# Order of the work ahead of the first group of a four-layer attention kernel: weight loads without a wait, buffer clears moved, step list rewritten

## What is computed

```python
x = L0(x, ctx)   # normalise rows, project with Wn, Wm, Wl (64x64) and biases bn, bm, bl; softmax over 256 positions;
                 # Wo, bo; + x
x = L1(x, ctx)   # layer norm of ctx (gamma, beta), Q K V, 16 heads of 16, softmax over 64, Wo, times tanh(gate), + x
x = L2(x, ctx)   # the same with its own weights
x = L3(x, ctx)   # q = x Wq^T, k, v from ctx, one head of 256, softmax over 64, Wo, times alpha, + x
```

## Time and profile before

| | before |
|---|---|
| median of 3 runs | 714.7 us (714.55 to 716.21) |
| profiled execution, device time | 714.7 us |
| its span in the profile | 712.5 us |
| PE busy | 652.5 us (92%) |
| PE weight loads busy | 578.6 us (81%) |
| DVE busy | 494.7 us (69%) |
| ACT busy | 463.4 us (65%) |
| POOL busy | 203.7 us (29%) |

### The profile page before, as it was taken

How to read it: one execution, slowest core, us unless ns; L and a number is a source line. 1 busy time by engine, 2 the same in 40 slices (tenths; PEclk the granted TensorE clock), 3 DMA queues, 4 the chain that set the end, 5 groups by cost and what they waited for, 6 DMA issues and landing times.

```text
span 712.5 us, 21646 instructions
## 1 busy us (share of the span) xinstructions
PE 652.5 (92%) x8643; PEld 578.6 (81%) x8643; DVE 494.7 (69%) x1083; ACT 463.4 (65%) x893; POOL 203.7 (29%) x169
## 2 busy tenths in 40 slices
PE   2988999989999899989999899998999899998985
PEld 1867898778988799878987789877988789987884
DVE  5857687675777657685776757867577857765575
ACT  1886575865847666665757658486575666676571
POOL 6333610426006250145203370061601533021100
PEclk9999999999999999999999999999999999999999
DMA  6320000200002000200003000020001100000000
GB/s 154 119 63 2 3 2 2 95 2 2 2 31 65 1 2 2 93 4 2 2 2 94 2 2 2 20 77 2 2 2 48 48 2 1 2 33 2 2 2 30
DMA packets 18491, 18.18 MB, mean 26 GB/s; under 512 B 1829, under 2 KB 18341, under 8 KB 18405
## 3 DMA queue, kind: packets, MB, share of 16 engines
q1 hardware_dynamic: 17504, 16.42, 7.3%
q0 software_dynamic: 320, 0.26, 0.4%
q10 hardware_dynamic: 580, 0.14, 0.1%
HBM read 12.63 MB, written 4.19 MB: 24 GB/s over the span
## 4 chain that ended last, share of the span: by engine, by line
PE 45%; issue 26%; POOL 12%; ACT 8%; DVE 4%; DMA 3%; ACTq 1%; SPq 1%; POOLq 0%; DVEq 0%
PE psum L352 7%; PE psum L561 7%; PE psum L354 6%; PE psum L353 5%; PE psum L581 4%; PE psum L634 4%; POOL kbd L1113 3%; ACT work L755 3%; PE psum L437 2%; POOL x_norm L1154 2%; ACT work L741 2%; POOL c_norm L1154 2%; PE psum L627 2%; PE psum L571 1%; ACT v L694 1%
## 5 line engine op out<-in xcount | busy, mean ns | idle before, releaser
L1113 POOL TENSOR_TENSOR kbd<-k_tmp,own_row 128x1024 f32<-128x1024 f32 x32 | 60.6, 1893 | 400.4 <-ACT k_tmp L689 400.4
L922 DVE TENSOR_REDUCE negmax<-psum 128x8 f32<-128x512 f32 x128 | 87.6, 684 | 35.2 <-PE psum L561 35.2
L755 ACT ACTIVATE work<-psum,group_mask 128x512 f32<-128x512 f32 x128 | 80.2, 688 | 28.0 <-PE psum L581 27.8
L926 DVE TENSOR_TENSOR shifted<-psum,negmax 128x512 f32<-128x512 f32 x128 | 88.5, 692 | 8.0 <-ACT work L741 2.9
L741 ACT ACTIVATE work<-shifted 128x512 f32<-128x512 f32 x128 | 77.6, 632 | 13.8 <-DVE shifted L926 13.5
L581 PE MATMUL psum<-const,work 64*128 64x64 f32 x1536 | 67.0, 228 | 17.8 <-ACT work L741 15.6
L581 PEld LDWEIGHTS psum<-const,work 64*128 64x128 f32 x1536 | 55.6, 139 | 32.7 <-issue 29.3
L561 PE MATMUL psum<-kbd,work 64*128 64x128 f32 x1024 | 71.5, 282 | 3.9 <-POOL kbd L1113 2.1
L634 PE MATMUL psum<-v,work 128*64 128x34 f32 x2048 | 69.2, 225 | 5.7 <-ACT work L755 5.7
L634 PEld LDWEIGHTS psum<-v,work 128*64 128x64 f32 x2048 | 64.2, 138 | 12.0 <-issue 10.7
L561 PEld LDWEIGHTS psum<-kbd,work 64*128 64x128 f32 x1024 | 61.7, 188 | 10.7 <-ACT work L706 2.8
(11 more groups left out here) (182 smaller groups left out, 1705.9 us busy)
## 6 DMA issues: line engine op xcount, KB each, us to landing
x_raw<-in_x_dram SPq DMA_DIRECT2D x8, 512.0 KB, 3.9
c_raw<-in_ctx_dram SPq DMA_DIRECT2D x8, 512.0 KB, 4.7
out_dram<-attn SPq DMA_DIRECT2D x16, 256.0 KB, 2.7
mrow_u<-in_mask_dram SPq DMA_DIRECT2D x8, 64.0 KB, 4.6
work<-in_L_xattn_Wq_dram SPq DMA_DIRECT2D x2, 256.0 KB, 4.1
work<-in_L_xattn_Wk_dram SPq DMA_DIRECT2D x2, 256.0 KB, 4.4
work<-in_L_xattn_Wv_dram SPq DMA_DIRECT2D x2, 256.0 KB, 5.0
work<-in_L_xattn_Wo_dram SPq DMA_DIRECT2D x2, 256.0 KB, 6.0
```

The source lines that it names most:

```text
L755: act.activation(probsT[:, slot, :], o[:], ACT.Copy, scale=group_mask[:, i:i + 1]).then_inc(free, 1)
L922: dve.tensor_reduce(negmax[:, i % 2, :], sv, AX_X, ALU.max, negate=True).then_inc(rowmax, 1)
L926: dve.tensor_tensor(shifted[:, i % 2, :].rearrange("t (j k) -> t j k", k=C), sv, negmax[:, i % 2, :].unsqueeze(2).broadcast_to([P, NJ, C]) ...
L1113: pool.tensor_tensor(kbd[l - 1][:, i], k_tmp[:, i, :].rearrange("p (b s) -> p b s", s=C).unsqueeze(2).broadcast_to(each), own_row[:].unsqu ...
```

## The change

Four things are changed, all in the start. SP no longer waits at L331. ACT's queue issues the four weights of layer 0 ahead of the three bias rows. DVE clears `v2`, `probs3` and `v0` at its very beginning, directly behind `w0_bd`, and not behind `MV`. And `PROLOGUE` lists the same steps in another order, which also gives many steps another bank.

```diff
-    o = p("MT") + [("ST", 0)] + p("GT") + [("ST", 1)] + [("ST", 2)] + p("MS") + [("ST", 3)] + [("MV", 0)] + f("xT", 0)
-    o += [("WB", 0)] + [("NB", 0)] + f("cT", 0) + f("cT", 1) + p("Wq1", "Wk1") + [("NM", 1)] + [("TG", 0)] + p("W0T")
-    o += [("NM", 0)] + p("Wv1", "Wo1") + f("xT", 1) + p("Wq2") + f("nT", 0) + f("nT", 1) + f("Mn", 0) + p("Wo3T")
-    o += f("Mn", 1) + p("Wk2", "W0", "Wv2", "Wo2") + f("Mm", 0) + [("KB", 1)] + p("M3") + f("V0", 0) + f("V0", 1)
-    o += [("KB", 2)] + f("Mm", 1) + p("VW3", "VB2", "VB1") + [("OB", 1)] + [("OB", 2)]
+    o = p("MT", "MS") + [("ST", 0)] + [("ST", 1)] + f("cT", 0) + f("xT", 0) + [("ST", 2)] + [("ST", 3)] + [("MV", 0)]
+    o += p("GT") + f("xT", 1) + [("WB", 0)] + p("Wq1", "Wk1") + [("NB", 0)] + [("TG", 0)] + f("cT", 1) + p("W0T", "Wv1")
+    o += [("NM", 1)] + p("Wq2", "Wk2") + [("NM", 0)] + p("Wo1", "Wv2", "W0") + [("KB", 1)] + f("nT", 0) + f("nT", 1)
+    o += p("Wo2", "Wo3T", "M3") + f("Mn", 0) + f("Mn", 1) + f("Mm", 0) + f("V0", 0) + [("KB", 2)] + p("VB1") + [("OB", 1)]
+    o += f("Mm", 1) + f("V0", 1) + p("VW3", "VB2") + [("OB", 2)]
...
             load_group(0)
-            sp.wait_ge(w0_bias_loaded, 3 * 16)
-            sp.wait_ge(w0_loaded, 4 * 16)
             for n in "qkvo":
...
+            for i, n in enumerate(("Wn", "Wm", "Wo", "Wl")):
+                act.dma_start(w0_raw[:, i, :], w[f"L0_xattn_{n}"].unsqueeze(0).broadcast_to([2, C, C])).then_inc(w0_loaded, 16)
             for i, n in enumerate(("bn", "bm", "bl")):
...
-            for i, n in enumerate(("Wn", "Wm", "Wo", "Wl")):
...
             dve.memset(w0_bd, 0.0).then_inc(w0_ready, 1)
+            for t in (v2[0], v2[1], probs3):
+                dve.memset(t[:], 0.0)
+            dve.memset(v0[:, :, :, C], 1.0).then_inc(cleared, 1)
...
                     moments_step(None)
-                    clear_values()
```

More of the change, by code:

```diff
@@ L825, in _ @@
                               w[f"L0_xattn_{n}"].unsqueeze(0).unsqueeze(0).broadcast_to([1, 2, C])).then_inc(w0_bias_loaded, 16)
-            for i, n in enumerate(("Wn", "Wm", "Wo", "Wl")):
-                act.dma_start(w0_raw[:, i, :], w[f"L0_xattn_{n}"].unsqueeze(0).broadcast_to([2, C, C])).then_inc(w0_loaded, 16)
             for step in PROLOGUE:
@@ L1053, in iteration @@
                         moments_step(g)
-            def clear_values():
-                for t in (v2[0], v2[1], probs3):
-                    dve.memset(t[:], 0.0)
-                dve.memset(v0[:, :, :, C], 1.0).then_inc(cleared, 1)
-                dve.wait_ge(cleared, 1)
-                for t in v2:
-                    for h in range(2):
-                        dve.memset(t[C * h:C * h + C, :, :, h, VW - 1], 1.0).then_inc(cleared, 1)
-            dve.memset(w0_bd, 0.0).then_inc(w0_ready, 1)
+            dve.memset(w0_bd, 0.0).then_inc(w0_ready, 1)
+            for t in (v2[0], v2[1], probs3):
+                dve.memset(t[:], 0.0)
+            dve.memset(v0[:, :, :, C], 1.0).then_inc(cleared, 1)
+            dve.wait_ge(cleared, 1)
+            for t in v2:
+                for h in range(2):
+                    dve.memset(t[C * h:C * h + C, :, :, h, VW - 1], 1.0).then_inc(cleared, 1)
             dve.wait_ge(mask_loaded, 16)
```

## The result

| | before | after |
|---|---|---|
| median | 714.6 us (714.34 to 716.21, 4 runs) | 722.1 us (721.12 to 726.43, 4 runs) |
| ratio to before | | 1.0113, 95% interval 1.0077 to 1.0151 |
| profiled execution, its span | 714.7 us, 712.5 us | 722.0 us, 720.0 us |

The change made the kernel slower by 1.1%; the prediction was 711.3 us, with a range from 710.0 to 717.0. What happened is the first rival, the starving bias rows, and further than its own end, 718.8.

What follows compares the result with a forecast made beforehand. Bound: ACT's queue in the start's second half, begun behind DVE's `norm_bias`. Normalisation 4.0 us sooner, ACT's work unchanged, bias rows costing 0.5, put T(0,0) 3.4 us sooner: 714.7 - 3.4 = 711.3 us, range 710.0 to 717.0.

Steps and rivals of the forecast that it cites:

- the first rival: Start, ACT's queue: SP's weights starve the bias rows and GT stands still; up to 718.8 us, chance 0.17.
- The frame: Whole kernel: the loop only shifts, so the time is T(0,0), PE's first L581, plus a constant.
- Bias rows: Start, end of ACT's queue: GT at 12.5, between 12.0 and about 20, costing 0.5 us.
- The rows: Profile before, 1.5 us of full q1: no q10 packet listed, leaning to q10 held off; up to 718.8 us.
- Weights: Start, SP's queue: without the wait PE has the first four weights at 12.5 instead of 18.5, upper end 14.4.
- later weights push the chain one for one: ACT ahead of the first normalisation at 17.9: weights later than about 12.9 delay it equally.
- The second rival, sluggish loads: Start: GT at 13.5 to 16, weights at 14 to 16, or gates 2 to 3 us later; 712.5 to 714.7, chance 0.22.
- Clears: DVE's start: clears end at 7.45, `mask_col` 1.0 us later at 8.15, 6.07 us freed behind MV.
- the rival of the clears that hold POOL's queue: Start: DVE's clears hold back POOL's issues, gates at about 11 to 12; 714.7 us, chance 0.04.
- The list collects both: Start: the new step order gathers what the clears and missing wait free; first normalisation 4.0 us sooner, at 17.9.
- The fourth rival: Start: weights no earlier than 18.4, four more ACT steps ahead; normalisation 23.5, exponentials 45.3, 716.3 us, chance 0.03.
- ACT's sum: ACT from first normalisation to exponentials: stays 21.75 us, 1.4 saved by earlier steps, 1.4 added by a second POOL wait.

Runs made afterwards that it cites:

- b_clears: The kernel before with only the clears moved to the beginning of DVE's queue; 714.9 us, 0.9981 of before.
- b_small_sp: The kernel before without SP's wait, bias rows and layer 0's weights issued by SP ahead of layer 1's weights; 715.1 us, 0.9985 of before.
- b_nowait: The kernel before with only SP's two waits removed; 720.0 us, 1.0058 of before.
- a_small_sp: The changed kernel with bias rows and layer 0's weights issued by SP ahead of its twelve weights; 713.9 us, 0.9981 of before.
- a_hold23: The changed kernel with SP's two waits put behind layer 1's four weights; 716.1 us, 1.0011 of before.
- a_w0late: a_small_sp with layer 0's weights issued by SP behind layer 1's and ahead of layer 2's; 714.3 us, 0.9977 of before.
- a_pool: The changed kernel with the three bias rows and layer 0's four weights issued by POOL instead of ACT; 712.9 us, 0.9967 of before.
- a_biasfirst: The changed kernel with ACT's queue in the old order, bias rows ahead of layer 0's weights; 721.6 us, 1.0082 of before.
- a_wait: The changed kernel with SP's two waits put back ahead of the twelve weights; 716.8 us, 1.0013 of before.
- a_ob: a_small_sp with the end of the step list changed: both VB side by side, both OB last; 712.9 us, 0.9966 of before.
- b_list: The kernel before with only the changed step list; 718.1 us, 1.0026 of before.
- a_w0late_ob2: a_w0late with the end of the step list changed so that POOL's first OB product runs under other steps; 712.7 us, 0.9949 of before.

## Why the prediction was wrong

- **The frame held, with a limit.** S(1,0) moved by 6.65 us and the time by 7.3. But T(0,0) is not the last point on which the start acts: from X to S(1,0) it is 17.22 us before, 17.42 in the changed kernel, 17.94 to 17.98 in b_clears, b_small_sp and b_nowait, where the granted clock fell below 1 behind a pause of PE. And from S(1,0) of group 1 to the end of the span it is between 566.8 us (a_small_sp) and 569.6 (a_hold23), 567.5 before and 568.7 after: 1.2 us of the 7.5 by which the span grew lie there. Nothing ties them to the change, and their cause stays open: it is 568.5 to 568.9 in eight of the other twelve kernels, whatever their start. The clock doesn't account for them. The windows view shows it for the last 20.5 us, in the changed kernel 0.85:

```profile
699.50:720.00 20.50, 13.24 (x132) 10.63 (x130) 9.96 (x28) 4.89 (x11) 0.00 (x0) 0.85 0.08 27
```

and before 0.94:

```profile
692.00:712.50 20.50, 13.17 (x148) 10.99 (x148) 10.46 (x30) 5.96 (x12) 0.00 (x0) 0.94 0.08 27
```

  but in a_w0late it was 0.95, with 568.6 us.

- **Bias rows: the step that failed.** I put GT at 12.5, between 12.0 and 20; it ran at 22.52. The working from that term to the exponentials was right: 39.7 + (22.52 - 12.0) = 50.2, 50.11 measured. The upper end was also too low: I let the rows land once q1 was empty, and dated that from q1 near its full rate, which it didn't keep (39.4% from 11 to 13 us). It still moved 107 packets from 20 to 22 us, when the last row landed. What the term left out is the work ahead of the rows on their own queue: four weights that are most of its 532 packets, of which ACT's queue moved some 30 per us beside SP's loads and not 115. That held ACT's issues too, 3.3 to 3.5 us each, so that the last bias row was issued at 15.01 only.
- **Which evidence to believe.** The rows showed no packet of q10 beside a full q1; I followed the rule of the Trainium skill (DMA: Bandwidth & Descriptors, section Queues, rings and completion order) that the engines go round the queues packet by packet. The rule was not what failed. By the estimate above, turns packet by packet on two engines give 60 packets in 2 us, and 57 came: the trace agrees with it where q1 is full. What failed is what I drew from it, that GT would stay near 12.5; I had counted neither the packets ahead of the bias rows nor the engines that they use. The row pointed the right way but proved less than it seemed: in the same 1.5 us of the changed kernel (4.5 to 6.0) q10 moved 65 packets beside q1 at 87.4%, since its weights had been issued earlier. That rows and outcome agree is in part luck. I gave the row 0.17.
- **Weights.** Taken 12.5, upper end 14.4; the four had landed at 15.9 (the fourth issued at 4.31, 11.6 us to landing). In a_pool, where GT came at 13.81, PE had them by 14.90, and in a_biasfirst at 15.30, for which it had waited 2.59 us. The second rival, sluggish loads, was thus true as well, for the weights and nearly so for the gates, 1.8 us late where it said 2 to 3. The rest of this step held: "later weights push the chain one for one", 12.9 for 17.9, is a distance of 5.0 us from W1 to NM 1, and it was 4.97, 5.06, 5.04, 5.05 and 5.17 us in the changed kernel, a_wait, a_hold23, a_small_sp and a_pool (4.59 in a_ob). With the seven small transfers out of the way the change comes to 712.9 us (a_pool), 0.3% better than before where I forecast 0.5%; its interval just takes in both, but its exponentials came at 41.60 and not at 40.2.
- **Clears.** They ended at 7.5 as said. The gates came at 8.88 and not 7.04 (the copy waited 1.17 us for them), `mask_col` at 9.02 and not 8.15, so the cover was thinner than taken. POOL's issues kept their 0.5 us: the rival of the clears that hold POOL's queue is out.
- **The list.** "The list collects both" found no support: the list costs some 2 us with weights at 18.1 to 18.4, and a_small_sp, which has it and the moved clears, is behind b_small_sp by 1.3 us in X, with weights at 16.7 to 16.9. No run sets the old list beside it with weights at 13 to 15. The fourth rival had this loss right (24.35 and 45.85 in b_list for its 23.5 and 45.3), but the steps that the list adds ahead of NM 1 are three, the prediction's own tanh, Wv1 and xT 1, and not four. ACT's sum was well priced (21.5 us for 21.75, two waits of 1.39).
- **Not foreseen:** ACT was shut in its own queue until 15.60, so that DVE waited for `cT_hi` and MV ran from 19.74 to 20.38, where I had it end at 13.8:

```profile
17.60 0.69 DVE L880 TENSOR_TENSOR cT_lo<-psum,cT_hi 128x512 fp32r<-128x512 f32 x1 [5.00 <-ACT cT_hi L674]
...
19.74 0.64 DVE L996 BATCH_NORM_AGGREGATE mean_var<-stats 128x2 f32<-128x6 f32 x8
```
  Had GT come at 12.5, this would have been the next wait; a_biasfirst, where ACT was free only at 15.19, doesn't separate the two, as layer 0's weights were later still.

Between X and T(0,0) the changed kernel took 0.4 us more (2.22 us for 1.79). From 47 to 52 us its granted clock was 0.66, behind a wait of PE, which may account for it.

```profile
47.78 0.38 PE L350 MATMUL psum<-wT_v_hi,nT_hi 128*128 128x256 f32 x1 [2.30 <-DVE mm_lo L887]
```

## What to carry to other kernels

A small load that the next step needs should not stand behind many small packets on one hardware queue while another hardware queue runs bulk loads: put it on the same queue ahead of the bulk (a_small_sp), or on POOL's (a_pool), and keep an engine that is needed soon from issuing transfers at all. A wait that looks like lost time on a queue engine may be what keeps another queue alive; before it goes, ask which transfers were let through by it. And price a list together with its loads: this one cost some 2 us with weights at 18 us, and no run shows it paying with earlier ones.

## What the hardware showed that I had not expected

- Beside SP's 256 KB loads, ACT's queue moved 31 to 82 packets in each 2 us from 5 to 17, and 231 alone, while SP's own queue was at 39 to 102% of the engines. At full q1 that is what fair turns on some two engines would give (60, the estimate above). The lows down to 31 it doesn't account for. That the mean share of the 16 engines was as low as 62% then (11 to 13) does not show room, since single engines are not listed. In a_w0late the same loads on SP's own queue, with ACT's empty, held an issue of SP for 4.53 us: one queue is enough to hold an issue.
- An issue is not always cheap: 0.4 to 0.6 us where little is under way, but 3.1 to 5.4 us for two or three of ACT's beside SP's twelve weights (5.38 us in a_biasfirst), and 4.53 us on SP in a_w0late, for the third small weight behind four large ones. Up to 2.77 us (a_wait, for `Wl`) it took on ACT even with SP held back by the wait. The engine does nothing else meanwhile.
- DVE's two copies of WB took 0.58 us in a_small_sp, 0.76 in a_w0late_ob2, 1.69 in a_w0late and 2.66 in b_clears, where POOL's 128x512 operations ran beside them. The same instructions can so cost 2 us more by a shift of their neighbours.
